# Two-layer graph attention block in fp32 on one core: the transpose of z in batches 2 to 12 made by VectorE in 32x32 blocks and sixteen SBUF-to-SBUF transfers in place of TensorE

## What is computed

```python
def gat(inp, mask, W, a):                       # one attention layer
    h = inp @ W
    e = leaky_relu(h @ a[:F] [:, None] + h @ a[F:] [None, :], 0.2)
    att = softmax(where(mask > 0, e, -9e15))
    return elu(att @ h)

h   = relu(layernorm(x))
o1  = relu(h @ mlp1_w + mlp1_b)                 # 512 x 256
z   = elu(gat(o1, None, W_fc, a_fc)) + o1       # first attention, no mask
o2  = relu(z @ mlp2_w + mlp2_b)                 # 512 x 128
x   = x + relu(elu(gat(o2, adj, W_hand, a_hand)) + o2)
h   = relu(layernorm(x))
out = x + gat(h, adj, W, a)
```

## Time and profile before

| | us |
|---|---|
| median of 3 runs | 432.83 (432.77 to 433.05) |
| span of the profiled execution | 429.0 |
| TensorE (PE) busy | 411.1, 96% |
| TensorE weight loads (PEld) busy | 352.7, 82% |
| VectorE (DVE) busy | 357.8, 83% |
| ScalarE (ACT) busy | 315.7, 74% |
| GpSimd (POOL) busy | 24.9, 6% |
| DMA, mean share of 16 engines busy | some 28% |

### The profile page before, as it was taken

One profiled execution on the slowest core, in us unless ns is written; L12 is line 12 of the kernel. 1 busy time (PEld: TensorE's weight loads), 2 busy tenths in 40 slices (PEclk: granted clock), 3 DMA queues, 4 the chain that ended last, 5 costly groups with the idle time before them and its releaser, 6 DMA issues.

```text
span 429.0 us, 8704 instructions
## 1 busy us (share of the span) xinstructions
PE 411.1 (96%) x2544; PEld 352.7 (82%) x2544; DVE 357.8 (83%) x1226; ACT 315.7 (74%) x764; POOL 24.9 (6%) x53
## 2 busy tenths in 40 slices
PE   6999999999999999999999999999999999989782
PEld 4688779887898899797998788989879799869772
DVE  7786588878998898988898868979698899889974
ACT  2655659658796787786878688687867887799774
POOL 0000000000001000010100000100000000000000
PEclk9999999999999999999999999999999999999997
DMA  7854323123423142232222213222320122120001
GB/s 209 278 146 130 105 74 121 74 76 98 125 98 75 53 138 84 52 101 74 75 82 68 75 53 98 79 72 74 80 87 10 49 93 59 45 80 24 27 1 57
DMA packets 39461, 36.42 MB, mean 85 GB/s; under 512 B 4080, under 2 KB 30320, under 8 KB 39408
## 3 DMA queue, kind: packets, MB, share of 16 engines
q1 hardware_dynamic: 37408, 33.17, 26.1%
q10 hardware_dynamic: 2000, 2.63, 1.8%
HBM read 31.46 MB, written 4.32 MB: 83 GB/s over the span
## 4 chain that ended last, share of the span: by engine, by line
PE 87%; DVE 5%; ACT 3%; issue 2%; DMA 1%; SPq 0%; POOL 0%; ACTq 0%; DVEq 0%
PE bank L1530 24%; PE bank L1437 23%; PE bank L1426 13%; PE bank L1416 6%; PE bank L1477 6%; PE bank L1455 6%; PE bank L1445 3%; PE bank L1538 2%; PE bank L1496 1%; PE bank L1466 1%; DMA row<-row_scratch 1%; DVE stats L1036 1%; DVE u L1265 1%; ACT ext L826 1%; ACT e L911 1%
## 5 line engine op out<-in xcount | busy, mean ns | idle before, releaser
L1530 PEld LDWEIGHTS bank<-ext,prob 128*128 128x128 f32 x1024 | 119.6, 192 | 6.3 <-issue 4.9
L1530 PE MATMUL bank<-ext,prob 128*128 128x129 f32 x1024 | 122.1, 275 | 0.3 <-DVE prob L1207 0.2
L1437 PE MATMUL bank<-ext,prob 128*128 128x257 f32 x512 | 119.0, 380 | 0.0
L1437 PEld LDWEIGHTS bank<-ext,prob 128*128 128x128 f32 x512 | 94.8, 190 | 17.3 <-issue 4.5
L1211 DVE SCALAR_TENSOR_TENSOR prob<-prob,square,mask_t 128x512 f32<-128x512 f32 x98 | 70.6, 739 | 0.9 <-ACT prob L859 0.8
L1426 PE MATMUL bank<-wfc_sb,o_t 128*128 128x259 f32 x256 | 64.0, 382 | 0.4 <-ACT o_t L790 0.4
L859 ACT ACTIVATE prob<-row,square 128x512 f32<-128x512 f32 x78 | 54.1, 720 | 0.1
L1426 PEld LDWEIGHTS bank<-wfc_sb,o_t 128*128 128x128 f32 x256 | 46.3, 190 | 9.6 <-issue 4.5
L903 ACT ACTIVATE y<-bank,recip 128x128 f32<-128x128 f32 x128 | 39.3, 369 | 15.3 <-DVE recip L1257 14.2
L911 ACT ACTIVATE e<-y,minus_one 128x512 f32<-128x512 f32 (+1 forms) x70 | 47.7, 688 | 1.4
L1265 DVE SCALAR_TENSOR_TENSOR u<-e,y 128x512 f32<-128x512 f32 (+1 forms) x70 | 44.1, 638 | 4.2 <-issue 2.2
(11 more groups left out here) (98 smaller groups left out, 499.1 us busy)
## 6 DMA issues: line engine op xcount, KB each, us to landing
row<-row_scratch SPq DMA_DIRECT2D x36, 256.0 KB, 3.3
moments_row<-moments_scratch SPq DMA_DIRECT2D x13, 512.0 KB, 3.8
x_in<-in_x SPq DMA_DIRECT2D x16, 256.0 KB, 5.3
x_res<-in_x SPq DMA_DIRECT2D x16, 256.0 KB, 4.6
out<-y_out SPq DMA_DIRECT2D x15, 256.0 KB, 3.9
normed<-in_x_t SPq DMA_DIRECT2D x14, 256.0 KB, 4.3
row_scratch<-square_t SPq DMA_DIRECT2D x144, 0.5 KB
adj_sb<-in_adj ACTq DMA_DIRECT2D x1, 1024.0 KB, 8.1
```

The source lines that it names most:

```text
L1437: last = nc.tensor.matmul(filled[:, 0:H + 1], gat1.targets(b, t, c), gat1.features_and_one(b, t), start=(t == 0), stop=(t == C - 1))
L1530: last = nc.tensor.matmul(filled[:, e * (D + 3):e * (D + 3) + D + 1], L.targets(b, t, c), L.features_and_one(b, t), start=(t == 0), stop=( ...
```

## The change

For batches 2 to 12 (`MOVED`), steps 4 and 5 above are made in another way. The other five batches keep them.

- TensorE's steps `z_0` and `z_1` of these eleven batches are gone from its list.
- New on VectorE, `turnu_0` and `turnu_1` (L1308): each half of `u` (128x512) is transposed in 32x32 blocks into a new tile `u_turned`. That puts each block's features on 32 partitions, but on the partition group a of its nodes.
- New on SyncE, `move` (L689): sixteen DMAs inside SBUF, one for each pair of source partition group a and target group q, 32 partitions x 2 x 128 elements, 32 KB each. They put the blocks where they belong, into `z_t`. Before them SP waits for both halves of `u_turned` and for `mlp2` of two batches ago (the slot of `z_t`).
- VectorE's `z_0`, `z_1` (L1316) wait for all sixteen to land and add `o1_t` in place, SBUF with SBUF. The nodes of `z_t` lie in the order (a, c, i), and `mlp2` reads them back as (c, a, i) by its access pattern, in runs of 32 elements.
- `u_turned` has one buffer: `turnu_0` of a batch waits for the move of the one before.
- The -1 of elu leaves the addition. In its place, once at the start, TensorE sums w2 over its rows (`sums_w2`: two matmuls of one column) and VectorE subtracts the sums from the second bias; the first `mlp2` on ScalarE waits for that.
- The whole table `ORDER` is new, on all five engines.

```diff
+MOVED = tuple(range(2, 13))
...
+            def move_blocks(b):
+
+                sp.wait_ge(*u_blocks.at(b, 2))
+                if b.first > 1:
+                    sp.wait_ge(*o2_filled.two_back(b))
+                for a in range(ROWS):
+                    for q in range(ROWS):
+                        sp.dma_start(z_t[32 * q:32 * (q + 1), b.slot, :, a * P:(a + 1) * P],
+                                     u_turned[32 * a:32 * (a + 1), :, q].rearrange("p k c i -> p k (c i)")).then_inc(
+                            z_moved.sem(b), 16)
...
+            def turn_blocks(b, part):
+
+                r = slice(part * C // 2, (part + 1) * C // 2)
+                dve.wait_ge(*s1.u.at(b, part + 1))
+                earlier = [n for n in MOVED if n < b.n]
+                if part == 0 and earlier:
+                    dve.wait_ge(*z_moved.landed(Batch.nth(earlier[-1])))
+                nc.vector.transpose(u_turned[:, :, :, r].rearrange("p k q c i -> p c (k q) i"),
+                                    gat1.u[:, r].rearrange("p c (k i) -> p c k i", i=32)).then_inc(u_blocks.sem, 1)
+
             def residual1(b, f):
+                if moved(b):
+                    dve.wait_ge(*z_moved.landed(b))
+                    z = z_t[:, b.slot, f].rearrange("p (a c i) -> p a c i", a=ROWS, c=C)
+                    o1 = o1_t[:, b.of(O1_DEPTH), f].rearrange("p (c a i) -> p a c i", a=ROWS, c=C)
+                    nc.vector.tensor_tensor(z, z, o1, ALU.add).then_inc(z_ready.sem, 1)
+                    return
                 dve.wait_ge(*z_filled.at(b, f + 1))
                 if b.first > 0 and f == 0:
                     dve.wait_ge(*o2_filled.two_back(b))
-                nc.vector.scalar_tensor_tensor(out=z_t[:, b.slot, f], in0=bank_of(f"z_{f}", b)[:], scalar=-1.0,
-                                               in1=o1_t[:, b.of(O1_DEPTH), f], op0=ALU.add, op1=ALU.add).then_inc(
-                    z_ready.sem, 1)
+                nc.vector.tensor_tensor(z_t[:, b.slot, f], bank_of(f"z_{f}", b)[:], o1_t[:, b.of(O1_DEPTH), f],
+                                        ALU.add).then_inc(z_ready.sem, 1)
...
+            def sums_w2(b):
+
+                pe.wait_ge(s_w2, 16)
+                filled = free("sums_w2", b)
+                for k in range(HT):
+                    last = nc.tensor.matmul(filled[:, 0:1], w2_sb[:, k], score_scale[:, 1, 0:1],
+                                            start=(k == 0), stop=(k == HT - 1))
+                last.then_inc(s_w2_sums, 1)
...
                 for k in range(HT):
-                    last = nc.tensor.matmul(filled[:], w2_sb[:, k], z_t[:, b.slot, k],
+                    z = by_blocks(z_t[:, b.slot, k]) if moved(b) else z_t[:, b.slot, k]
+                    last = nc.tensor.matmul(filled[:], w2_sb[:, k], z,
                                             start=(k == 0), stop=(k == HT - 1))
```

Of the table, SyncE's line in batch 9's neighbourhood, before and after:

```diff
-        row1.10 result.4 load_again.7 row3.6 row0.14 row2.8 load_again.8 row2.9 row3.7 row0.15 row1.11 row2.10
+        row0.14 move.8 load_again.8 row1.10 row3.6 move.9 row0.13 row2.8 move.10 result.4 row2.9 row3.7 row1.11
```

More of the change, by code:

```diff
@@ L475, in gnn_program @@
         o1_ready = signal("o1_ready", HT)
-        z_filled = signal("z_filled", HT)
+        u_blocks = signal("u_blocks", 2, without=[n for n in range(B) if n not in MOVED])
+        z_moved = slots("z_moved", [n for n in range(B) if n not in MOVED], ROWS * ROWS)
+        z_filled = signal("z_filled", HT, without=MOVED)
         z_ready = signal("z_ready", HT)
@@ L555, in gnn_program @@
             "scores23": lambda b: (s_wa, 9),
+            "sums_w2": lambda b: (s_b2, 1),
         }
```

341 lines of the change are left out of this document (176 added, 165 removed).

## The result

The changed kernel takes **491.54 us** (median of 4 runs, 489.55 to 493.24) against 432.8 in the same comparison (431.69 to 433.05): a ratio of 1.137, 95% interval 1.133 to 1.141. The prediction was 425.3, its range ended at 434.5. The kernel is 59 us slower.

A forecast was written before the change was run, and what follows sets the result against it. TensorE, without idle time from 60 to 356 us, was taken as the bound: 429.0 - 9.7 (transposes) + 0.2 (sums_w2) + 2.0 (VectorE density) = 421.5 us span, plus 3.8 for the median: 425.3; range 422.0 to 434.5.

The forecast's parts named there:

- Queued behind a move are rows of other attentions, which it can delay by up to 7 us ... I cost this at nothing.: SP's queue: attention rows issued behind a move could be up to 7 us late; priced at nothing.
- the length of the move: SP's sixteen DMAs, from issue to last landing: 5.9 to 10.2 us, taken as 7.5.
- The estimate of 15 us: The move's sixteen transfers one after another at the skill's 0.95 us for 64 KB; set aside because small DMAs overlap.
- Rival 3: VectorE's wait ahead of the additions: move late, TensorE runs dry, kernel slower at 436 us; chance 0.13.
- Its rule for the stall: VectorE's additions: each stall is the move's length less the work between; at 10.2 us, some 21 us together.
- What is taken from TensorE is won: TensorE, 60 to 356 us without idle time: eleven batches lose 22 x 0.44 = 9.7 us of transposes, all gained.
- The durations: VectorE: block transpose 0.70 us by record, 0.62 occupied, 13.7 us more work in all; additions 677 against 674 ns.
- Rival 4: VectorE's block transpose costs more than an element at a time; at 1.2 us each, 439 us; chance 0.07.
- The 2.0 us lost: Stage from 60 to 356 us: VectorE reaches 92.7% density, not the needed 93.3%, so 2.0 of the 9.7 us go.
- Rival 2: VectorE becomes the bound at 90.7% density: stage 294.8 us, time 431.6 us; chance 0.15.
- `mlp2` on runs of 32 elements: TensorE's read of z in runs: same 1.72 us for both feature tiles; a tenth slower would lose 1.9 us.
- The tail: From 356 us on, batches 11 to 15, chain through VectorE, ScalarE and a row's DMA: left at 73 us.

The follow-up runs named there:

- experiment 4: Kernel before, own table, plus sixteen tiny SP transfers for each of batches 2 to 12, waited for by no compute engine: 478.03 us against 431.85, ratio 1.107.
- experiment 7: Kernel before, own table: bias alone 433.42 us; bias without TensorE's transposes 428.56; 22 unused block transposes behind u 438.86; both parts 441.41; before 431.89.
- experiment 8: Kernel before with 22 unused block transposes later in VectorE's list: 434.29 us against 432.65; also without TensorE's transposes: 435.32 against 431.85.
- experiment 6: Changed kernel, sixteen tiny transfers into a spare tile, issued in four parts with a step of SP's table between where it fits: 497.80 us, ratio 1.153.
- experiment 3: Changed kernel with sixteen tiny transfers per move into a spare tile, the additions not waiting for their landing: 487.74 us, ratio 1.127.

## Why the prediction was wrong, step by step

The error is 66 us. The move makes 55 of it (491.54 - 436.86), and the other 11.6 are what the kernel without transfers lies above the forecast (436.86 - 425.3). The move failed in two terms, its delay of rows and its length.

**The first step that failed: "Queued behind a move are rows of other attentions, which it can delay by up to 7 us ... I cost this at nothing."** The mechanism was named and its price left out. Measured, the issuing costs 51 us in the changed kernel without the additions' wait (487.74 - 436.86), and 46 in the kernel before (478.03 - 431.85, experiment 4), there with some 20 of them from one pair of moves. The reason given, that VectorE issues the row's own transpose behind the additions, was found at one place, batch 9's, and taken for all. It holds behind two of the eleven moves, those of batches 7 and 9. Behind eight others the row's write starts ahead of the additions, as at the move shown above: turned at 198.30, written at 204.93, the delay of up to 7 us that the prediction named.

**The second: the length of the move** was 7.5 us with 10.2 as the upper end; it is 12.3 for batch 6, with 10.2 to 11.1 of issuing in the eleven and 1.9 from an issue to its landing. The mis-sized term is the issue: 0.31 to 0.43 us read off transfers with memory on one side, 0.64 to 0.69 in the move. So the bound was none: the rows that I took it from had another kind of transfer. The estimate of 15 us that the prediction worked out from a figure of the Trainium skill and set aside (DMA: Bandwidth & Descriptors, section Measured) came nearer than the 7.5. That is luck, since the figure is for transfers from HBM issued by GpSimd and counts the time of the DMA engines, not of the queue. The argument against it, four small DMAs issued and landed in 2.2 us, shows that landings overlap, and issues don't.

**Rival 3** was right in direction and in its row (waits of VectorE for the DMA into z_t over 10 us: 39.6). Its rule for the stall was right too: with 12.3 us in place of 10.2 the work between leaves 6.4 us in batch 9 and 3.0 to 5.0 in nine others, an estimate of some 42 us, and the eleven waits are 39.6 (the longest, 5.9, in batch 3). Its price, 436, was far too low, because half was taken to fall into idle time. Behind each of nine moves TensorE loses 4.8 to 7.8 us, more than VectorE waits. And the place is not the only one: with these waits taken away 487.7 us remain. It looked only at the engine that waits for the move, not at what else stands in the queue that makes it. The runs don't divide the 55 us between the two paths. They overlap, and what stands behind the move in SP's queue gives 51 alone.

**"What is taken from TensorE is won"** failed too. 9.7 us of transposes gone give 3.3 us with the bias and 4.9 against it (experiment 7), from a stage at 296.00 of 296.00. Over the span the matmuls' busy time falls by 5.8 us (411.1 to 405.3) and the weight loads' by 9.1 (352.7 to 343.6). A span full of pipelined records doesn't show that each instruction starts as early as it could; the two joints that I looked at the earlier trace rows were tight, and the stage as a whole was not. The Trainium skill (Trainium Kernel Development and Optimization, section Best Practices) says to judge the distance from the limit by the weight loads' busy share and not by the matmuls'. The trace agrees: weight loads stood at 82%, where matmuls stood at 96%.

**VectorE.** The durations were right: the block transpose has 696 ns by its record, the addition between SBUF tiles 688, and VectorE is busy 370.9 us, 13.1 more than before.

```profile
L1308 DVE STREAM_TRANSPOSE u_turned<-u x22: 666/696/711, 73.2 to 367.0; 128x512 f32<-128x512 f32 x22
```

Rival 4 is out. The 2.0 us lost were mis-sized as a matter of density: by density VectorE can carry the work (1.6 us in experiment 8), right behind u it costs 7.0. That this is because z and the rows' args stand behind the pair fits the two runs, but no trace was read for it. Rival 2 thus named a number (431.6) that was better than mine for the change without transfers, with a reason that the runs don't bear out.

**Small terms.** `mlp2` on runs of 32 elements takes 1.88 us as before, so nothing was right. The tail is as predicted: behind the last move the matmul records stay some 53 us later than those of the kernel without transfers, and nothing is added. The bias and `sums_w2` were 0.2; measured 0 to 2 us (ratio 1.000 to 1.005). SP's added issuing was 66 us; it is 116.6.

**The sum, in the trace.** Between the kernels without transfers and with sixteen the spans differ by 489.1 - 436.4 = 52.7 us. TensorE's idle time grows from 25.0 to 60.6 us, 35.6 of it. The other 17.1 us are the same 2460 records, busy for 428.5 instead of 411.4 us, with a granted clock of 0.953 over the span instead of 0.991; the four of `mlp2` at 206.33, 3.78 us together, are among them. Compared one by one, 44 records take over 1.5 times as long as in the kernel without transfers, 18.2 us more in all, and 30 of them are `mlp2`'s. So about a third of the loss is not waiting but work that ran at the lower of the two clock levels (1.2 instead of 2.4 GHz) after a wait. No term of the prediction had this, and it needs rows of a stalled TensorE, which the kernel before doesn't have.

What stays open: what the late landing alone would cost, whether a hold in many small parts would cost less than a whole (experiment 6 has a wait of its own), and why both parts together lose what each alone promises.

## What to carry to other kernels

A queue that issues DMAs is an engine with its own budget: price an added transfer by its issue time on that queue and by every step behind it, above all where the queue carries a short chain that all others wait for (here the softmax row). An in-order queue gives some slack for nothing, and how much depends on what stands behind: in the new table 5 us in each batch cost little and 8 us cost 26 us in all, while in the old one a single hold of 10 us cost nothing at four places and two in close succession cost 20. Taking work from the busiest engine is worth its duration only if leaving that work out, in the real order, shows it; that is one run, and it comes before building the replacement.

## What the runs showed of the hardware

- A DMA with SBUF on both sides costs its queue about 0.6 us (SP 594 ns, ScalarE 618, GpSimd 536), with memory on one side 427 ns on SP, nearly independent of its size from 16 to 256 KB and of its partitions from 16 to 128 (46 issues, 489 to 758 ns). In the moves of the kernel it is 0.64 to 0.69 on SP from one start to the next, and 0.53 on GpSimd.
- Tiny transfers of 1 KB took as long to issue and to land (10.2 to 11.4 us for sixteen in experiment 3, 1.8 us) as those of 32 KB (10.2 to 11.1, 1.9).
- After 5.18 us of idle time TensorE took 3.78 us for four matmul records that take 1.88 elsewhere, and the attention behind them 4.30 us for sixteen that otherwise take 3.63. The granted clock in these stretches of the changed kernel, with TensorE idle for most of the 6 us ahead and busy in the 8 and the 6 us behind:

```profile
200.00:206.00 6.00, 1.15 (x6) 0.48 (x4) 1.40 (x4) 0.49 (x2) 0.00 (x0) 0.87 0.32 87
206.00:214.00 8.00, 7.67 (x20) 5.02 (x21) 6.65 (x18) 4.53 (x9) 0.35 (x1) 0.67 0.40 123
214.00:220.00 6.00, 6.00 (x54) 5.97 (x54) 3.58 (x16) 4.44 (x13) 1.20 (x2) 1.00 0.28 94
```
